# Preln attention layer on eight cores: normalization roots ahead of evictions, chunks 2 and 3 transposed by DMA, later column maxima and second layer

## The reference, cut to what matters

```python
# x: (8, 4096, 1024) f32, W: (1024, 1024), b: (1024,), weight: (1024, 1024)
n = layernorm(x)                                   # over the last axis, eps 1e-5
f = einsum('bsd,hd->bsh', n, W) + b
e = einsum('bih,bjh->bij', f, f) + clip(|i-j|, 0, 10) * 0.01
x = x + einsum('bij,bjh->bih', softmax(e), f)
scale = max(mean(|weight|), 1e-5)
wt = clip(round(weight / scale), -1, 1)
x = x + einsum('bsi,oi->bso', layernorm(x), wt * scale)
```

## Time and profile before

| | us |
|---|---|
| median of 3 runs | 971.85 |
| lowest, highest | 971.29, 983.76 |
| the profiled execution, its own time | 970.58 |
| its span, first to last instruction, slowest core | 968.9 |
| spans of the eight cores | 959.4 to 968.9 |
| TensorE busy | 938.1 (97%) |
| VectorE busy | 566.4 (58%) |
| ScalarE, GpSimd busy | 334.5 (35%), 311.6 (32%) |

### The profile page before, as it was taken

The page is one execution under the profiler, slowest core; times in us unless marked ns, Lnnn a source line. Parts: engine busy times, 40 slices in busy tenths (PEclk is TensorE's granted clock), DMA queues, the critical chain, the costliest instruction groups (busy, mean ns, idle before and its releaser), DMA issues.

```text
span 968.9 us, 15189 instructions; the slowest of 8 cores (959.4 to 968.9 us)
## 1 busy us (share of the span) xinstructions
PE 938.1 (97%) x4767; PEld 456.9 (47%) x4767; DVE 566.4 (58%) x857; ACT 334.5 (35%) x471; POOL 311.6 (32%) x336
## 2 busy tenths in 40 slices
PE   7799989999999999999999999999999999999998
PEld 6464434444444444544444444444444444444443
DVE  6566688888887778432433444444454455565643
ACT  3555544333333354334342332222213213122110
POOL 4111212121222223000111233244354365575760
PEclk9999999999999999999999999999999999999999
DMA  8467698496888369796798999999999997867422
GB/s 274 162 157 213 169 280 226 146 255 173 184 218 230 117 183 236 237 264 196 211 227 214 229 223 207 227 218 227 245 200 204 228 221 194 236 174 198 147 57 76
DMA packets 230074, 195.81 MB, mean 202 GB/s; under 512 B 136910, under 2 KB 200682, under 8 KB 228074
## 3 DMA queue, kind: packets, MB, share of 16 engines
q1 hardware_dynamic: 146170, 79.99, 37.1%
q10 hardware_dynamic: 68432, 63.44, 26.8%
q0 software_dynamic: 15392, 51.40, 16.8%
HBM read 108.79 MB, written 53.49 MB: 167 GB/s over the span
## 4 chain that ended last, share of the span: by engine, by line
PE 71%; DVE 16%; DMA 8%; issue 3%; ACT 1%; DVEq 1%; SPq 0%; ACTq 0%; POOL 0%; POOLq 0%
PE pb L791 38%; PE pb L464 13%; PE pb L853 11%; DMA ln2T<-ln 6%; PE pb L400 6%; DVE rm L498 4%; DVE cmax L505 4%; PE pt L284 2%; DVE st L321 1%; DVE st L323 1%; DVE lnb L350 1%; DVE wqb L959 1%; DMA ln1Ta<-lnb 1%; DVEq L62 1%; DMA ln1Tb<-lnb 1%
## 5 line engine op out<-in xcount | busy, mean ns | idle before, releaser
L464 PE MATMUL pb<-fT 128*128 128x512 bf16 (+3 forms) x1152 | 238.1, 362 | 2.4 <-ACT fT L410 1.3
L791 PE MATMUL pb<-f,pTb 128*128 128x512 bf16 x1024 | 232.9, 380 | 0.0
L791 PE MATMUL pb<-f,pTa 128*128 128x512 bf16 x1024 | 230.2, 379 | 0.0
L464 PEld LDWEIGHTS pb<-fT 128*128 128x128 bf16 x1152 | 110.4, 98 | 121.8 <-issue 4.8
L791 PEld LDWEIGHTS pb<-f,pTa 128*128 128x128 bf16 x1024 | 99.8, 99 | 114.1
L791 PEld LDWEIGHTS pb<-f,pTb 128*128 128x128 bf16 x1024 | 99.9, 99 | 111.7
L500 POOL DMA_DIRECT2D escr<-er x128 | 70.8, 556 | 253.6 <-ACT er L490 146.7
L803 DVE SCALAR_TENSOR_TENSOR o<-pb,st,xres 128x512 f32<-128x512 f32 x64 | 48.0, 751 | 138.3 <-PE pb L791 138.3
L490 ACT COPY er<-pb 128x512 f32<-128x512 f32 (+2 forms) x128 | 70.1, 547 | 129.9 <-PE pb L464 40.5
L744 POOL TENSOR_TENSOR acc<-acc 128x128 f32<-128x128 f32 (+6 forms) x90 | 108.7, 1207 | 13.5 <-POOL acc L744 0.9
L498 DVE TENSOR_REDUCE rm<-er 128x1 f32<-128x512 f32 (+2 forms) x128 | 81.5, 637 | 22.4 <-ACT er L490 10.1
(11 more groups left out here) (107 smaller groups left out, 692.2 us busy)
## 6 DMA issues: line engine op xcount, KB each, us to landing
escr<-er POOLq DMA_DIRECT2D x105, 256.0 KB, 3.6
xres<-x POOLq DMA_DIRECT2D x32, 512.0 KB, 9.4
out<-outb SPq DMA_DIRECT2D x31, 512.0 KB, 8.0
xb<-x SPq DMA_DIRECT2D x28, 512.0 KB, 5.9
wst<-wt SPq DMA_DIRECT2D x8, 512.0 KB, 15.7
wst<-ft SPq DMA_DIRECT2D x8, 512.0 KB, 7.2
escr<-eB POOLq DMA_DIRECT2D x15, 256.0 KB, 2.4
eB<-escr ACTq DMA_DIRECT2D x2, 1920.0 KB, 13.2
```

The lines of the kernel that those rows point to most:

```text
L464: inst = e.matmul(bk[:, 0:n], fT[:, h * S + I * P:h * S + (I + 1) * P], fT[:, h * S + c0:h * S + c0 + n], start=(h == 0), stop=(h == NH - 1))
L791: inst = e.matmul(bank[bav[nb]][:, :], pT[I % 2][:, j * P:(j + 1) * P], f_sb[:, j * D + nb * 512:j * D + (nb + 1) * 512], start=(pos == 0) ...
```

## The change

In the head, `ln_rs` and `ln_apply` of tiles 4 to 7 come earlier between the projections, the projections of chunk 0 are split into halves further (0, 1 and 2), the transposes of tile 3 are evicted by ScalarE and not by VectorE, and the band is made after `ln_apply(7)`. `xtrans` takes the DMA from tile 8 on, not from 16; the applies and transposes of tiles 8 to 15 get other places, and so do the f transposes of chunk 0, two of the loads and the quantization steps. In the second part, `mfin_col`, `mfin4`, `csum`, `mrow_store` and `mrow_load` come later, all `mfin4` use bank MC, and `ffn` with `final` moves from position 7 to 13.

```diff
@@ -244,19 +244,22 @@
             col(STD), col(EPSC), AF.Ln, bias=col(EPSC), scale=1.0), t_eps)
         t_idb = DVE.op(lambda e, w: e.tensor_copy(idb[:, :], idf[:, :]))
 
-
         fband2 = at(R_ER, BWID, F32, "band2")
-        DVE.op(lambda e, w: e.tensor_scalar(
-            band[:, :], band[:, :], col(ROWB), -float(MAXD - 1),
-            ALU.subtract, ALU.add))
-        DVE.op(lambda e, w: e.tensor_scalar(
-            fband2[:, :], band[:, :], -1.0, float(MAXD), ALU.mult, ALU.add))
-        DVE.op(lambda e, w: e.tensor_scalar_add(
-            band[:, :], band[:, :], float(MAXD)))
-        DVE.op(lambda e, w: e.tensor_tensor(
-            band[:, :], band[:, :], fband2[:, :], ALU.min))
-        DVE.op(lambda e, w: e.tensor_scalar(
-            band[:, :], band[:, :], 0.0, -BSCALE, ALU.max, ALU.mult))
+
+        def emit_band():
+
+            DVE.op(lambda e, w: e.tensor_scalar(
+                band[:, :], band[:, :], col(ROWB), -float(MAXD - 1),
+                ALU.subtract, ALU.add))
+            DVE.op(lambda e, w: e.tensor_scalar(
+                fband2[:, :], band[:, :], -1.0, float(MAXD), ALU.mult, ALU.add))
+            DVE.op(lambda e, w: e.tensor_scalar_add(
+                band[:, :], band[:, :], float(MAXD)))
+            DVE.op(lambda e, w: e.tensor_tensor(
+                band[:, :], band[:, :], fband2[:, :], ALU.min))
+            DVE.op(lambda e, w: e.tensor_scalar(
+                band[:, :], band[:, :], 0.0, -BSCALE, ALU.max, ALU.mult))
+            er_free[0] = (DVE.last(),)
 
 
         def warm(n):
@@ -360,11 +363,11 @@
             k, pos = s % 2, s % 4
             dst = ln1T[s // 4 % 2].rearrange("p (c x) -> p c x", c=NH)[
                 :, :, pos * P:(pos + 1) * P]
-            if s >= 16:
+            if s >= 8:
                 xtr_tok[s] = ln1T_tok[s] = tdma(
                     sl_xt[k], dst, lnb[k][:, :], apply_tok[s],
                     fproj_pe[s // 4 - 2])
-                if s < NST - 4:
+                if 16 <= s < NST - 4:
                     x_load(s + 4)
                 return
             srcs = [lnb[k][:, j * P:(j + 1) * P] for j in range(NH)]
@@ -541,7 +544,7 @@
         def mfin4(g):
 
             q = g + 1
-            bk, free = (MB, mb_free) if g in (5, 3) else (MC, mc_free)
+            bk, free = MC, mc_free
 
             def pe(e, w):
                 inst = None
@@ -1010,67 +1013,67 @@
         fproj(0, 0, 0)
         xtrans(2)
         fproj(0, 1, 0)
-        xtrans(3, DVE)
+        xtrans(3)
+        ln_stats(4)
+        fproj(0, 2, 0)
         fproj(0, 0, 1)
-        fproj(0, 1, 1)
-        ln_stats(4)
-        fproj(0, 2)
         ln_rs(4)
         ln_apply(4)
         ln_stats(5)
-        fproj(0, 3)
+        fproj(0, 1, 1)
+        fproj(0, 2, 1)
         xtrans(4)
         ln_rs(5)
         ln_apply(5)
+        fproj(0, 3)
         fproj(0, 4, 0)
         xtrans(5)
+        ln_stats(6)
         fproj(0, 4, 1)
-        ln_stats(6)
-        fproj(1, 0, 0)
-        fproj(1, 1, 0)
         ln_rs(6)
         ln_apply(6)
         ln_stats(7)
+        fproj(1, 0, 0)
+        fproj(1, 1, 0)
+        xtrans(6)
         fproj(1, 2, 0)
-        fproj(1, 3, 0)
-        xtrans(6)
-        fproj(1, 4, 0)
         ln_rs(7)
         ln_apply(7)
+        emit_band()
+        fproj(1, 3, 0)
+        fproj(1, 4, 0)
+        xtrans(7)
         fproj(0, 5)
-        xtrans(7)
         fproj(0, 6)
         fproj(0, 7)
         for k in range(3):
             ln_stats(8 + k)
         fproj(1, 0, 1)
+        egroup(0, 0)
         fproj(1, 1, 1)
-        egroup(0, 0)
+        egroup(1, 0)
         fproj(1, 2, 1)
-        egroup(1, 0)
         fproj(1, 3, 1)
-        fproj(1, 4, 1)
         ln_stats(11)
         egroup(2, 0)
+        fproj(1, 4, 1)
         ftrans(0, 0)
         ftrans(0, 1)
-        fproj(1, 5)
-        ftrans(0, 2)
-        ftrans(0, 3)
         ln_rs(8, 4)
         ln_apply(8)
         ln_apply(9)
+        xtrans(8)
+        xtrans(9)
+        fproj(1, 5)
+        egroup(3, 0)
+        ln_apply(10)
+        ln_apply(11)
+        xtrans(10)
+        xtrans(11)
         fproj(1, 6)
-        ftrans(0, 4)
-        ftrans(0, 5)
-        egroup(3, 0)
-        xtrans(8)
-        ln_apply(10)
+        ftrans(0, 2)
+        ftrans(0, 3)
         fproj(1, 7)
-        ftrans(0, 6)
-        ftrans(0, 7)
-        xtrans(9)
-        ln_apply(11)
 
 
 
@@ -1095,11 +1098,9 @@
             if c + 2 < NCH:
                 s0 = 4 * c + 8
                 if c == 1:
-                    when = [0, 1, 2, 3, 6, 7, 8, 11, 13]
-                    at_slot(0, lambda: xtrans(10))
-                    at_slot(1, lambda: xtrans(11))
-                    for k, i in enumerate((10, 12, 14, 15)):
-                        at_slot(i, lambda k=k: xtrans(s0 + k))
+                    when = [0, 1, 2, 3, 6, 6, 7, 10, 11]
+                    for h in range(4, NH):
+                        at_slot(h - 4, lambda h=h: ftrans(0, h))
                 else:
                     when = [int(n * v) for v in (
                         0, .06, .12, .18, .33, .38, .45, .52, .59)]
@@ -1108,25 +1109,24 @@
                 at_slot(when[4], lambda: ln_rs(s0, 4))
                 for k in range(4):
                     at_slot(when[5 + k], lambda k=k: ln_apply(s0 + k))
-                    if c > 1:
-                        at_slot(when[5 + k], lambda k=k: xtrans(s0 + k))
+                    at_slot(when[5 + k], lambda k=k: xtrans(s0 + k))
 
             for c_, i, fn, k in (
                     (1, 9, ft_load, 0), (1, 12, ft_load, 1),
                     (1, 15, ft_load, 2), (2, 0, ft_load, 3),
-                    (2, 4, ft_load, 4), (2, 8, ft_load, 5),
-                    (2, 12, ft_load, 6), (2, 16, ft_load, 7),
+                    (2, 4, ft_load, 4), (2, 13, ft_load, 5),
+                    (2, 15, ft_load, 6), (2, 17, ft_load, 7),
                     (2, 4, absum, 0), (2, 8, absum, 1), (2, 12, absum, 2),
                     (2, 16, absum, 3), (3, 1, absum, 4), (3, 4, absum, 5),
                     (3, 10, absum, 6), (3, 12, absum, 7),
-                    (3, 17, quant, 0), (3, 20, quant, 1), (4, 5, quant, 2),
+                    (3, 20, quant, 0), (3, 22, quant, 1), (4, 5, quant, 2),
                     (4, 9, quant, 3), (4, 19, quant, 4), (4, 23, quant, 5),
                     (5, 20, quant, 6), (5, 25, quant, 7)):
                 if c == c_:
                     at_slot(i, lambda fn=fn, k=k: fn(k))
             if c == 3:
                 at_slot(13, scale_sum)
-                at_slot(15, scale_prep)
+                at_slot(18, scale_prep)
 
             a, b = {2: (0, 6), 3: (6, 14), 4: (14, 22), 5: (22, 33),
                     6: (33, 48)}.get(c, (0, 0))
@@ -1199,23 +1199,24 @@
                 at_mark(0, 26, lambda: (lmm(I), rl(I)))
                 at_mark(*((1, 8) if pv > NST - 5 else (0, 18)),
                         lambda: ln2_trans(pv))
+            if I == NST - 2:
+                at_mark(0, 4, mrow_store)
             if I + 2 < NST:
-                at_mark(0, 7, lambda: (ffn(I + 2), final(I + 2)))
+                at_mark(0, 13, lambda: (ffn(I + 2), final(I + 2)))
             if nx >= 0:
-                at_mark(0, 26, lambda: csum(nx))
+                at_mark(*((1, 30) if first else (0, 26)), lambda: csum(nx))
             if nn >= 0:
                 if first:
-                    at_mark(0, 17, lambda: (mfin_col(nn, last_cm[0]),
+                    at_mark(0, 24, lambda: (mfin_col(nn, last_cm[0]),
                                             mfin_tmp(nn)))
-                    at_mark(0, 19, lambda: mfin_col(nn - 1, last_cm[0]))
+                    at_mark(0, 26, lambda: mfin_col(nn - 1, last_cm[0]))
                     for g, pos in zip(range(6, -1, -1),
-                                      (21, 23, 25, 27, 34, 39, 44)):
+                                      (30, 35, 40, 45, 50, 55, 60)):
                         at_mark(*divmod(pos, 32), lambda g=g: mfin4(g))
-                    at_mark(1, 18, mrow_store)
                     at_mark(1, 2, lambda: loadE(28))
                     at_mark(1, 22, lambda: wq_load(6))
                 if nn >= NST - 4:
-                    at_mark(0, 28, lambda: mfin_row(nn))
+                    at_mark(0, 29 if first else 28, lambda: mfin_row(nn))
                 at_mark(1, 24 if first else 2, lambda: sub(nn))
                 at_mark(1, 21 if first else 14, lambda: exp_row(nn))
             for nb in range(2):
@@ -1229,7 +1230,7 @@
                     ln2_stats0(nb)
             if nn >= 0:
                 ptrans(nn)
-            if first:
+            if I == NST - 2:
                 for g in range(6, 2, -1):
                     mrow_load(g)
             elif nn >= 16 and nn % 4 == 0 and nn < NST - 4:
```

## The result

The changed kernel takes 986.08 us in the median of its runs (979.18 to 1069.48), the kernel before 977.83 on the same chips (969.09 to 1063.04). The ratio of after to before is 1.0085, with a 95% interval of 1.0054 to 1.0116: about 8 us slower. The ratios, and the medians given under the experiments, leave out executions in which one die ran slow. The forecast of 968.2 is a ratio of 0.996 to the 971.85 shown before it, so the change is small, as forecast, but of the other sign; and 986.08 lies outside the stated 955 to 981. About 6 us of the distance in the absolute time is the kernel before itself, whose median moved from 971.85 to 977.83. A second timing of the same file, further down, gave 1.0108 (1.0075 to 1.014). The profiled execution of after took 982.4 us, that of before 970.58, so the two profiles differ by 11.8 us, more than the ratio says.

The account below looks back on a forecast made before the run. TensorE, busy 938.1 of 968.9 us, bounds the kernel. Terms +7.4 - 4.4 - 1.0 - 3.9 - 1.2 = -3.1 take 970.58 to 967.5, or 968.8 as a median; it says 968.2, range 955 to 981.

Parts of the forecast that it names:

- 44.1: 4.1 us earlier: Head, tiles 4 to 7: the new order ends fproj(0, 5) to (0, 7) near 44.1, 4.1 us earlier.
- Term: -1.0: Scale: scale_prep three slots later removes TensorE's wait of 1.04 on an eviction, -1.0 us.
- the terms for chunk 4 and the scale: Chunk 4: idle 2.7 and slow clock 1.7 go, -4.4 us; scale_prep later saves its wait, -1.0.
- rival B: Chunks 2 and 3: x loads ahead of the transposes hold the lnb ring longer; 975.1 at 22 us; chance 0.30.
- idle above 12 us: Sign of rival B: TensorE idles above 12 us before fproj(2, 0), where the forecast had 9 us.
- I take 18.2: Chunk 2 by DMA: the chain of applies and transposes takes 18.2 us, from rows of 18.4 and 18.3 in chunks 4 and 5.
- stand ahead of the first transpose on SP ... which pushes up: Chunk 2: x_load(12) and (13) precede the first transpose, lengthening the chain; f transposes now behind act on the other side.
- Term: +7.4: Chunk 3 by DMA: stall of 5.0 and 1.7 slow; first projection at 100.6 against 93.22, +7.4 us.
- B's rule: Chunks 2 and 3: each us on the chain counts twice, once a chunk.
- Each cycle is ... about even: Column maxima: mfin4 cycles in one bank about match the 1.08 between them, leaving 0.6 of waits; term -3.9 us.
- All of this ring moves with ffn, so its length stays: Second layer: ffn at 13 keeps four of five ln2T waits; 1.2 of the longest, 1.9, goes; term -1.2 us.

Follow-up runs that it names:

- the output later: The changed kernel with row 31's first-half output queued on VectorE behind all mfin4 maxima: ratio to before 1.0047 (1.0008 to 1.0086).
- chunks on TensorE: The changed kernel with transposes of tiles 8 to 15 and everything placed for them back as before: ratio to before 0.9938, 964.78 us.
- both mended by DMA: The changed kernel with chunks 2 and 3 still by DMA, x loads behind each chunk's transposes, row 31's first output later: ratio to before 0.9888, 962.39 us.

## Why the prediction was wrong

**What held.** The places were right, and so was the mechanism for the head, the chunks 2 to 4 and the scale. The head: "44.1: 4.1 us earlier" stands against 42.9, 5.3 earlier, or 4.5 in the median of the cores (43.3 and 47.8). TensorE waits for ln1Ta until 73.5 and for ln1Tb until 105.9, with a slower clock behind each. The wait for cmax at 387 is gone. So is the wait at the matmul of scale_prep, 0.3 to 2.9 us on the eight cores of before and nowhere in after, as "Term: -1.0" said (on seven of the eight it was VectorE's sums that were waited for, not an eviction). The wait ahead of chunk 4 shrinks from 1.59 to 1.04, and from its start to that of chunk 5 the lead over the slow stretch comes: with the slow clock behind chunk 3 counted into the term before it (105.92 to 110.7 holds 4.78 us at 0.50, a loss of 2.4), the delay falls from 15.1 to 11.4 by the start of chunk 5 (183.47 against 172.09). That is 3.7, where the terms for chunk 4 and the scale, which both lie in this stretch, made 5.4. And rival B, to which 0.30 was given, is the case that came true, with its sign, "idle above 12 us": loads ahead of the transposes stretch the chain, and from 19.8 on the change is slower.

**The step that failed first: "I take 18.2".** The chain measured 21.9 us in chunk 2 (51.55 to 73.4) and 22.5 in chunk 3 (83.3 to 105.8). It was read off chunks 4 and 5, where each load stands behind the transpose of its tile. The prediction saw the difference ("stand ahead of the first transpose on SP ... which pushes up"), and set against it that the f transposes had moved away, as if the two were equal. They aren't. With each load behind the transpose of its tile, as in the rows, the chain here is 14.2 where the rows had 18.4, so the quieter queue was worth about 4 us; the loads' places in the change cost 7.7 on top of that (21.9), and against no load beside the transposes at all 12.0, by bytes and by order of issue. Which transfers the 4 us come from wasn't parted. "Term: +7.4" measured +12.7 at the start of chunk 3's first projection, and 2.4 more behind it. Rival B at a chain of 22 us was priced at 975.1. Set beside 970.58 that is +4.5, and the profile shows +11.8, or +9.7 in the median of the cores. The working itself holds up to chunk 5 once the chain is the measured one. In the median of the cores the chain is 20.75; B's rule, 7.4 and twice the surplus over 18.2, makes 12.5, of which 1.7 is the slow clock behind the start. So chunk 3 would start 10.8 later, measured 10.7, and chunk 5, after the 5.4 of the next two terms, 7.1 later, measured 7.1. From there to the second part 2.5 us were added that no term forecast. Behind that the forecast was -2.6 up to the first feed-forward matmul, and the medians measured +4.4: this is the second step that failed. From that matmul to the end it was -2.5, measured -3.3.

**The second step: "Each cycle is ... about even", -3.9 for the column maxima.** The cycle was worked out from TensorE's and VectorE's own durations. What else stands in VectorE's queue between the groups was left out: row 31's first output, which waits for residual rows that were issued at 399.3 and landed 12.9 to 14.3 us later. One cycle took 8.4 us (405.88 to 414.32). From the start of the second part to the first feed-forward matmul it was +4.8 (+4.4 in the median) and not -2.6 (-3.9 and the 1.3 of the later place). With the output later that step is 40.0, -1.4 against the median of before (41.4) or -2.7 without the later place: most of the gain that the term meant is there once nothing stands ahead of the reductions.

**"All of this ring moves with ffn, so its length stays": -1.2 for the second layer.** Here the size was nearly right. Without the 1.3 of the later start the medians give -2.0, in after and with the place at 13 alone, and the ratio of the latter is 0.997. Both have 0 to 0.9 us of waits for ln2T on a core, where before had 0.3 to 4.0, so the ring doesn't keep its length, though the change timed again has 2.8 and 3.7 on two of its cores; that the transfers land sooner at 13 isn't clear of the spread between cores, and why the waits go wasn't shown. The term was read off the core with the most of these waits.

**The head, 4.1 us to the end.** It is 4.5 us where it is made (4.7 to 5.3 on the slowest cores), and 0.35% of the time, about 3.4 us, at the end of the head alone. The sum treated the terms as if none could eat another; about 1 us was eaten, and at which waits isn't shown.

**Where the time went.** On the slowest cores the +11.9 is: +5.1 up to chunk 2 and +7.6 up to chunk 3, both waits for the transposes with the clock behind the first; -1.3 up to chunk 5, which is the slow clock behind the second wait less the stalls that went; +2.6 up to the second part; +4.8 at the maxima; -6.9 in the second layer. In the medians the same six are +4.9, +5.8, -3.6, +2.5, +4.4 and -3.3. The +2.5 between chunk 5 and the second part has no experiment of its own. The runs bear out the parts: chunks on TensorE takes 1.5 to 1.7% off, the output later 0.4 to 0.6%.

**Which theory fell.** That the ring of two buffers sets the chain: four buffers gave 15.6 to 18.4 us, two with the loads in the same place 13.5 to 16.1. That SyncE's queue alone is what the loads block: with them on GpSimd's queue it stayed at 18.7 to 22.7. What stands is that plain loads in flight between a transpose's issue and its landing stretch that landing from 3.1 to between 5.2 and 9.3 us, and up to 12.5 with the loads issued by GpSimd, and that loads which wait for an apply hold back the transposes queued behind them.

**What stays open.** Why DMA transposes with short landings, which take 3.5 us of work from TensorE, give no shorter time than the transposes on TensorE (0.9888 and 0.9892). The late transpose behind the wait of 10.5 us, on one core of the version with both mended by DMA, left at 436.2 and landed 36.3 us later; it was seen once and not explained. Of the loads' 12 us, bytes and order of issue were parted in one execution of each. The moved loads, quantization steps and scale_prep were never tried by themselves.
